# Expert results added into token rows by GpSimd's accumulating DMA, in place of stores and a gather at the end

## The chip, the cores and the metric

The kernel runs on one core of one Trainium2 chip. The metric is device time in microseconds, from the start to the end of one launch. Five engines share the work: TensorE (PE), VectorE (DVE), ScalarE (ACT), GpSimd (POOL) and SyncE (SP), which here only issues DMAs.

## The reference

One layer: 2048 tokens (16 tiles of 128) of width 512. Gated cross attention comes first, then a feed-forward part, a mixture of eight experts with widths 256 to 1024 and two experts per token:

```python
h = x @ down_w + down_b                        # 512 -> 256
probs = softmax(x @ router_w + router_b - COST_LAMBDA * cost)
topv, topi = top_k(probs, 2)
gate = softmax(topv)
for k in range(2):
    for e in range(8):                         # only the token's own expert sees h, the others see 0
        hm = h * (topi[..., k] == e)
        acc += gelu(gelu(hm) @ w1[e] + b1[e]) @ w2[e] + b2[e]
    out += acc * gate[..., k]
out += 0.1 * (gelu(gelu(h) @ shared_w1 + shared_b1) @ shared_w2 + shared_b2)
out = out @ up_w + up_b + gelu(x) @ core_w + core_b
```

What an expert gives for a zero row is a constant, so the kernel runs each expert only on its own tokens and adds the constants by a small matrix product.

## The kernel before, in words

Every product is made of three float16 matmuls (`three`, L1124: high by high, high by low, low by high), which stand for one in float32. The order of the work on each engine is written out by hand in lists (`seq`), and engines wait for each other on semaphores whose values are planned ahead (`Tally.plan`, `wait`). Each engine and each DMA queue works in order: what stands behind a waiting instruction waits too.

**Attention** fills the first 380 us and is not changed.

**Rounds** (about 380 to 511 us). Four rounds `r`, each of four tiles of tokens. A round computes h, the logits, the top two, the gates `gat` (`g1`, `g2`), the matrix of gates `Gp` (`G`, L1544), the shared expert, and `core`. ACT copies the gelu of h of each tile as a float16 row (high and low halves, 1024 bytes; `row`, L1384), and POOL scatters each tile's rows twice, once for each of a token's two experts, into the table `g_rows` in memory, sorted by expert (`sc`, L1847: two indirect DMAs per tile, eight per round). ACT copies the shared expert's result into `acc` (L1395), 16 tiles of 256 columns in SBUF. In rounds 0 and 3 two of the row buffers lie in the part of `acc` that this copy writes, so it waits until their scatters have landed. In the last round DVE works out tables of where every block lies (`ro`, `wo`, `bo`, `flag`), and SP fills the ends of the experts' regions with zeros (L1079, L1082).

**Expert stage** (511.8 to 732.7 us). 42 half blocks `j`: 256 rows of one expert by up to 512 of its hidden columns. SP loads a block transposed (`load`, L1093), up to three ahead, into four buffers `XA`. PE computes `hidden(j)` (24 matmuls of 256 columns into `EH`), ACT takes the gelu (L1431), POOL casts it to its high half (L1910), DVE subtracts to get the low half (L1745), and PE computes `output(j)` (24 matmuls of 256 columns into `Y`). PE's order is hidden(j), output(j-1), hidden(j+1), output(j), and so on. DVE's `collect` (L1833) writes y to `ysb`, with the former half block added where both belong to one block (`flag`), and SP stores it to `y_rows` (L1104). In between DVE works out `places`, the row of `y_rows` that holds each token's result (`locate`), one small operation per half block, and SP loads back eight of the sixteen tiles of the residual (`xb_rows`, L1107).

**Final stage** (from 732.7 us). In four groups `g` of four tiles: POOL gathers for every tile the two expert rows of each token from `y_rows` (L1919: 32 indirect DMAs of 128 rows in all), DVE multiplies them by the gate and adds them to `acc` (`combine`, L1774), PE transposes `acc` (L1320, 8 transposes per group), ACT and DVE split it into halves (L1441, L1757), PE multiplies by `up_w` (24 matmuls of 512 columns per group, banks of `EH`), DVE adds the residual (L1765) and SP stores the tile to `out` (L1111). The gather buffers `yg` are four; the residual's last four tiles are loaded late, into buffers that group 1 used (L1115).

Of the kernel before, what the change touches and what calls it, by code (L numbers as in the profile page):

```python
# [20 lines left out]
F32 = mybir.dt.float32  # L21
# [7 lines left out]
P = 128  # L29
# [40 lines left out]
NCONST2 = 344  # L70
# [76 lines left out]
def constants():  # L147
# [17 lines left out]
    d[:, K2_BASE:K2_BASE + E] = REGION * np.arange(E)  # L165
    packed = [e + 8 * (HALVES[e] - 1) + 16 * HBASE[e] + 256 * FIRST[e] for e in range(E)]
# [646 lines left out]
def ffn(nc, c, keep, sb, ps, sem, ends, x1s, us, bcol, b2, rw, rb, upb, coreb, const, out):  # L813
# [4 lines left out]
    gsc = nc.dram_tensor("g_rows", [DUMP + BLK, 2 * LAT], F16, kind="Internal").ap()  # L818
    ysc = nc.dram_tensor("y_rows", [NJ * BLK, LAT], F32, kind="Internal").ap()
# [20 lines left out]
    slots, places, gat = A("slots", [P, NG, 2, G4], U32), A("places", [P, NG, 2, G4], U32), A("gat", [P, NG, 2, G4])  # L840
    nf, nz, ni, nb = A("nf", [P, E]), A("nz", [P, E], I32), A("ni", [P, E], I32), A("nb", [P, E], I32)
    hc = A("hc", [P, 4, 16])
    ro, wo, bo, flag = A("ro", [P, NJ], I32), A("wo", [P, NJ], I32), A("bo", [P, NJ], I32), A("flag", [P, NJ])
    bcur = A("bcur", [P, 2, 8])
    zrow = zs[:, :].bitcast(F16)
# [7 lines left out]
    row_of = lambda r, i: rows[i] if i < 2 or r else acc[:, i - 2, :].bitcast(F16)  # L853
    sah = [b2s[:, :].bitcast(F16), A("sah1", [P, L], F16)[:, :]]
    sal = [A(f"sal{i}", [P, L], F16)[:, :] for i in range(2)]
    rows = [A(f"rows{i}", [P, 2 * LAT], F16)[:, :] for i in range(2)]
# [4 lines left out]
    rows += [acc[:, 3 * G4 + i, :].bitcast(F16) for i in range(2)]  # L861
# [8 lines left out]

    xl = [uf[:, k, :] for k in range(LB)] + [flat(v).bitcast(F32)[:, k * L:(k + 1) * L] for v in (guh, gul) for k in range(2)]
    yg = [gf_[:, 0, :], gf_[:, 1, :], flat(gh).bitcast(F32), flat(gl).bitcast(F32)]
# [19 lines left out]
    t_ys = [T(f"y_out{i}", 16) for i in range(2)]  # L892
    t_yg = [T(f"y_in{i}", 16) for i in range(4)]
    t_xl = [T(f"xb_in{i}", 16) for i in range(8)]
# [7 lines left out]
    route_c = ["e1", "g1", "g2", "G1", "G2", "G"]  # L902
    tables = ["nf", "nz", "ni", "nb", "H", "c1", "c2", "c3", "ex", "dx", "A", "M1", "r1", "M2", "r2", "pki", "D", "valid",
              "e", "h", "t", "f", "b", "sub", "ro0", "ro1", "ro2", "ro", "wo0", "wo", "bo0", "bo", "flag"]
    four = lambda name: [(name, k) for k in range(4)]

    def seq(engine, r):
# [3 lines left out]
        if r == 0:  # L911
# [3 lines left out]
                "act": [("h", 0), ("h", 1)] + four("gu") + four("guh") + [("a", 0), ("a", 1)] + four("row") + [("gt", 0), ("acc", 0), ("acc", 1)],  # L915
# [48 lines left out]
    for j in range(NJ):  # L964
        t_gt[j % 4].plan(j)
        t_ys[j % 2].plan(j)
# [984 lines left out]
```

## Time and profile before

| | us |
|---|---|
| median of 3 runs (lowest to highest) | 803.62 (802.78 to 804.75) |
| the profiled execution's own time | 796.31 |
| its span, first to last instruction | 794.5 |
| PE busy in the span | 714.3 (90%) |
| DVE, ACT, POOL busy | 539.0, 462.8, 456.9 |
| mean granted TensorE clock | 0.970 |

The profile is of one execution, and all rows quoted are from it. A row of the timeline or of the chain begins with its start in us from the span's start, and its length in us. A row of the windows has from:to and the length in us; then the busy us, with the number of instructions, of PE's matmuls, PE's weight loads, DVE, ACT and POOL; then the granted TensorE clock (1.00 is 2.4 GHz, 0.50 is 1.2 GHz), the mean busy share of the 16 DMA engines, and GB/s. A busy engine counts for the time only where the others wait for it; an idle engine costs nothing where another sets the pace.

### The profile page before, as it was taken

The numbers are of one execution on the slowest core, as the hardware profiler recorded it, in microseconds if no ns is written. First come the engines' busy times: TensorE is split into PE (matmuls) and PEld (weight loads), VectorE is DVE, ScalarE is ACT, GpSimd is POOL, SyncE is SP. The second block draws the span as 40 slices with busy tenths as digits, with TensorE's granted clock in tenths as the row PEclk, the third lists the DMA queues.
The fourth block names the chain that finished last, engine by engine and source line by source line (L and its number), as shares of the span: only waits on it lengthen the run. The fifth ranks groups of instructions, "written<-read, shape, count | busy, mean of one in ns | idle before, by whom it ended". The sixth has DMA issues, their size and how long they took to land.

```text
span 794.5 us, 20245 instructions
## 1 busy us (share of the span) xinstructions
PE 714.3 (90%) x6134; PEld 384.1 (48%) x6134; DVE 539.0 (68%) x816; ACT 462.8 (58%) x969; POOL 456.9 (58%) x526
## 2 busy tenths in 40 slices
PE   1799999999999999999889998999999999998276
PEld 0122232333333332234445455588888888887132
DVE  2989999999999999987545865634444343433374
ACT  1399999999999999987345354244433444333010
POOL 4647778888888888577877676222222222221670
PEclk9999999999999999999979989999999999999588
DMA  6635656665666565443415123635454443432355
GB/s 201 222 112 178 198 190 191 202 195 193 188 194 200 188 196 178 137 142 120 173 69 180 59 106 112 168 81 120 110 115 112 120 119 109 113 102 73 96 186 203
DMA packets 118461, 118.18 MB, mean 149 GB/s; under 512 B 58356, under 2 KB 88308, under 8 KB 118392
## 3 DMA queue, kind: packets, MB, share of 16 engines
q1 hardware_dynamic: 114744, 108.75, 44.8%
q0 software_dynamic: 3072, 8.39, 3.3%
q8 instruction: 41, 0.67, 0.3%
q14 instruction: 28, 0.23, 0.1%
q10 hardware_dynamic: 576, 0.13, 0.1%
HBM read 59.70 MB, written 46.40 MB: 134 GB/s over the span
## 4 chain that ended last, share of the span: by engine, by line
PE 66%; DVE 8%; issue 8%; POOL 7%; ACT 5%; DMA 4%; SPq 0%; ACTq 0%; DVEq 0%; POOLq 0%
PE EH L1124 22%; PE Y L1124 15%; PE pv L527 11%; PE ring L514 7%; DVE mx L648 4%; PE nat L502 4%; ACT P L588 3%; POOL gf L1919 1%; DVE statx L630 1%; PE ring L546 1%; PE Y L1228 1%; DMA gh<-y_rows,places 1%; DMA q_scratch<-qhl 1%; POOL g_rows L1847 1%; PE EH L1166 1%
## 5 line engine op out<-in xcount | busy, mean ns | idle before, releaser
L648 DVE TENSOR_REDUCE mx<-nat 128x2 f32<-128x1024 f32 x256 | 298.2, 1215 | 29.2 <-PE nat L502 27.6
L588 ACT ACTIVATE P<-ring 128x512 f32<-128x512 f32 x512 | 276.2, 606 | 17.8 <-PE ring L514 10.0
L1431 ACT ACTIVATE X<-EH,bcur 128x256 f32<-128x256 f32 x168 | 85.8, 560 | 131.6 <-PE EH L1124 131.6
L527 PE MATMUL pv<-P,VT 128*32 128x256 f32 x2048 | 157.6, 391 | 0.3
L1910 POOL CAST u<-X 128x512 f16<-128x512 f32 x84 | 51.5, 613 | 174.9 <-ACT X L1431 174.9
L514 PE MATMUL ring<-QS,KS 49*128 49x512 f16 x512 | 122.8, 391 | 14.7 <-ACT P L588 13.4
L502 PE MATMUL nat<-KS,QS 48*128 48x512 f16 x512 | 110.9, 396 | 23.6 <-DMA KS<-k_scratch 15.9
L1124 PE MATMUL EH<-XA,whi 128*128 128x256 f16 x672 | 116.9, 273 | 1.2 <-DVE XB L1675 1.0
L1124 PE MATMUL Y<-whi,u 128*128 x672 | 116.9, 273 | 0.3 <-DVE u L1745 0.3
L1745 DVE TENSOR_TENSOR u<-X,u 128x512 f16<-128x512 f32 x84 | 57.8, 688 | 69.7 <-POOL u L1910 69.7
L1124 PE MATMUL EH<-XA,wlo 128*128 128x256 f16 x336 | 91.6, 273 | 0.0
L1124 PE MATMUL Y<-wlo,u 128*128 x336 | 91.6, 273 | 0.0
L514 PEld LDWEIGHTS ring<-QS,KS 49*128 49x128 f16 x512 | 31.9, 93 | 119.0 <-ACT P L588 99.2
L527 PEld LDWEIGHTS pv<-P,VT 128*32 128x32 f32 x2048 | 43.8, 108 | 90.9 <-issue 44.5
L1833 DVE SCALAR_TENSOR_TENSOR ysb<-ysb,flag,Y 128x512 f32<-128x512 f32 x42 | 31.4, 748 | 63.6 <-PE Y L1124 63.6
L1124 PEld LDWEIGHTS EH<-XA,whi 128*128 x672 | 65.8, 98 | 9.6 <-issue 2.0
L1124 PEld LDWEIGHTS Y<-whi,u 128*128 128x128 f16 x672 | 65.8, 98 | 8.2 <-issue 0.6
L502 PEld LDWEIGHTS nat<-KS,QS 48*128 48x128 f16 x512 | 26.0, 94 | 34.6 <-issue 17.3
L1660 DVE TENSOR_TENSOR ul<-uf,uh 128x512 f16<-128x512 f32 x16 | 25.4, 1637 | 19.0 <-ACT uh L1357 19.0
L1124 PEld LDWEIGHTS Y<-wlo,u 128*128 128x128 f16 x336 | 32.9, 98 | 3.8
L1124 PEld LDWEIGHTS EH<-XA,wlo 128*128 x336 | 32.9, 98 | 3.8
L1441 ACT CAST uh<-EH 128x512 f16<-128x512 f32 x8 | 4.7, 586 | 51.1 <-PE EH L1320 51.0
(265 smaller groups left out, 1057.7 us busy)
## 6 DMA issues: line engine op xcount, KB each, us to landing
y_rows<-ysb SPq DMA_DIRECT2D x42, 256.0 KB, 2.1
XA<-in_wall SPq DMA_DIRECT2D x8, 800.0 KB, 4.7
u<-in_wall SPq DMA_DIRECT2D x8, 800.0 KB, 4.3
QS<-q_scratch SPq DMA_DIRECT2D x64, 96.0 KB, 2.3
KS<-k_scratch SPq DMA_DIRECT2D x64, 96.0 KB, 2.3
X<-in_x SPq DMA_DIRECT2D x16, 256.0 KB, 2.7
X<-in_ctx_kv SPq DMA_DIRECT2D x16, 256.0 KB, 3.7
q_scratch<-qhl SPq DMA_DIRECT2D x16, 256.0 KB, 2.1
```

Of the source, the lines that this page charges most:

```text
L502: m = pe.matmul(nat[k % 2][:, a, :], QS[i][r, g, n, q0:q0 + P], KS[i][r, g, n, :], start=True, stop=True)
L514: pe.matmul(ring[place[key] % 3][:, :], KS[i][r, g, n, lb * P:lb * P + P], QS[i][r, g, n, :], start=True, stop=True).then_inc(t_ring.sem, 1)
L527: m = pe.matmul(pv[32 * j:32 * j + 32, q], VT[i][:, lb, g, j, :], Pb[4 * (s % 2) + j][:, q], start=(lb == 0 and half == 0), stop=(lb == 3) ...
L546: m = pe.transpose(ring[place[key] % 3][:, n * P:n * P + P], ct[i][:, lb * P:lb * P + P], ident)
L588: act.activation(Pb[4 * (s % 2) + j][:, :], bank[:, :], ACT.Exp).then_inc(t_use.sem, 1)
L648: dve.tensor_reduce(mx[:, k // 8, :, k % 8], nat[k % 2][:, :, :], AX.X, ALU.max).then_inc(t_max.sem, 1)
L1124: m = pe.matmul(dst, l, r, start=first and n == 0, stop=last and n == 2, skip_group_check=skip)
L1431: m = act.activation(af[j % 2][:, tile, :], EH[j % 2][:, n, s * BLK:(s + 1) * BLK], ACT.Gelu, bias=bcur[:, j % 2, tile:tile + 1], scale=bc ...
L1660: m = dve.tensor_tensor(ul[:, i, :], uf[:, i, :], uh[:, i, :], ALU.subtract)
L1745: dve.tensor_tensor(al[j % 2][:, 2 * n:2 * n + 2, :], af[j % 2][:, 2 * n:2 * n + 2, :], ah[j % 2][:, 2 * n:2 * n + 2, :], ALU.subtract).th ...
L1833: dve.scalar_tensor_tensor(out=ysb[j % 2][:, :, :], in0=ysb[1 - j % 2][:, :, :], scalar=flag[:, j:j + 1], in1=EY[j % 2], op0=ALU.mult, op1 ...
L1910: pool.tensor_copy(ah[j % 2][:, 2 * n:2 * n + 2, :], af[j % 2][:, 2 * n:2 * n + 2, :]).then_inc(t_pool.sem, 1)
```

## The change

Rows in `g_rows` become 1088 bytes: the 1024 bytes of before, then 16 float32 numbers ("meta"): the token's gates for the eight experts in the first eight, and the token's own row number in the last. ACT copies the meta part into each row buffer (`meta`, after the four `row` copies; in round 0 also after `gt`), and the scatter waits for it. DVE writes the row numbers (`Gi`). The padding rows at the ends of the regions get gates of zero and row numbers of a dump area of 256 rows (`blank`, set in round 3).

A table `y_sums` in memory, one row of 256 float32 for each token and the dump area, is first filled with `acc` (the shared part), one store per round, the last one ahead of the first block's load in SP's queue. For each half block SP loads also the meta part of the 256 rows (64 bytes each), ACT copies the column of the block's expert to `gcur` (`gates`), DVE copies the row numbers to `to` and multiplies y by the gate (in place of adding the former half block), and POOL adds the 2 x 128 rows into `y_sums` by two indirect DMAs that accumulate. As two half blocks can hold the same token, the add of half block j begins only when that of j-1 has landed.

Gone are the stores to `y_rows`, `flag`, `places` and its 14 operations, the 32 gathers and `combine`. When the last add has landed, SP loads `y_sums` into `acc` by four plain loads of 512 KB, one per group. The transposes of group g+1 now stand ahead of the products of group g; the transposes have their own banks (`Y[0]`), the products all four banks of `EH`. All twelve tiles of the residual that need it are loaded during the expert stage.

```diff
+                m = act.copy(row_of(r, i).bitcast(F32)[:, LAT:LAT + META], Gp[:, i, 0:META])       # "meta"
 # scalar: order within a round
-                cur([("a", 0), ("a", 1)] + four("row") + [("gt", 0)] + four("guh") + [("acc", 0), ("acc", 1)])
+                cur([("a", 0), ("a", 1)] + four("row") + four("meta") + [("gt", 0)] + four("guh") + [("acc", 0), ("acc", 1)])
 # scalar: round 0
-  ... four("row") + [("gt", 0), ("acc", 0), ("acc", 1)],
+  ... four("row") + [("gt", 0)] + four("meta") + [("acc", 0), ("acc", 1)],
 # gpsimd, scatter
             if name == "sc":
+                wait(pool, t_act, r, "meta", i)
                 wait(pool, t_act, r, "row", i)
 # sync
+            def sums(r):
+                wait(sp, t_act, r, "acc", 1)
+                sp.dma_start(ysum[r * G4 * P:(r + 1) * G4 * P].rearrange("(t p) c -> p t c", p=P),
+                             acc[:, G4 * r:G4 * r + G4, :]).then_inc(t_as.sem, 16)
...
-                sp.dma_start_transpose(gT[j % 4], gsc[bass.ds(at, BLK), :]).then_inc(t_gt[j % 4].sem, 16)
+                sp.dma_start_transpose(gT[j % 4], gsc[bass.ds(at, BLK), 0:LAT].bitcast(F16)).then_inc(t_gt[j % 4].sem, 16)
+                if j >= 4:
+                    sp.wait_ge(t_gc.sem, t_gc.at[j - 4,])
+                    sp.wait_ge(t_to.sem, t_to.at[j - 4,])
+                sp.dma_start(meta[j % 4][:, :, :], blocks(gsc[bass.ds(at, BLK), LAT:LAT + META])).then_inc(t_mt[j % 4].sem, 16)
...
-                wait(sp, t_dve, "E", j, "y")
-                sp.dma_start(blocks(ysc[j * BLK:(j + 1) * BLK, :]), ysb[j % 2][:, :, :]).then_inc(t_ys[j % 2].sem, 16)
...
+            for i in range(2):
+                sp.wait_ge(t_ad[i].sem, t_ad[i].value)
+            for g in range(NG):
+                r = C_GROUPS[g][0] // G4
+                sp.dma_start(acc[:, G4 * r:G4 * r + G4, :],
+                             ysum[r * G4 * P:(r + 1) * G4 * P].rearrange("(t p) c -> p t c", p=P)).then_inc(t_al[g].sem, 16)
 # scalar, after the second gelu of each half block
+        def gates(j):
+            v = act.value_load(eo[0:1, j:j + 1], min_val=0, max_val=E - 1)
+            wait(act, t_mt[j % 4], j)
+            if j >= 4:
+                wait(act, t_dve, "E", j - 4, "y")
+            act.copy(gcur[:, j % 4, :].unsqueeze(2), meta[j % 4][:, :, bass.ds(v, 1)]).then_inc(t_gc.sem, 1)
 # vector
         def collect(j):
+            wait(dve, t_mt[j % 4], j)
+            if j >= 2:
+                wait(dve, t_ad[j % 2], j - 2)
+            dve.tensor_copy(to[:, j % 2, :], meta[j % 4][:, :, META - 1]).then_inc(t_to.sem, 1)
             wait(dve, t_pe, "E", j, "y")
-            if j >= 2:
-                wait(dve, t_ys[j % 2], j - 2)
-            if j >= 1:
-                wait(dve, t_dve, "E", j - 1, "y")
-            dve.scalar_tensor_tensor(out=ysb[j % 2][:, :, :], in0=ysb[1 - j % 2][:, :, :], scalar=flag[:, j:j + 1],
-                                     in1=EY[j % 2], op0=ALU.mult, op1=ALU.add).then_inc(t_dve.sem, 1)
+            dve.wait_ge(t_gc.sem, t_gc.at[j,])
+            dve.tensor_tensor(ysb[j % 2][:, :, :], EY[j % 2], gcur[:, j % 4, :].unsqueeze(2).broadcast_to([P, 2, LAT]),
+                              ALU.mult).then_inc(t_dve.sem, 1)
 # gpsimd
+            def add(j):
+                wait(pool, t_dve, "E", j, "y")
+                pool.wait_ge(t_to.sem, t_to.at[j,])
+                if j >= 1:
+                    wait(pool, t_ad[(j - 1) % 2], j - 1)
+                else:
+                    pool.wait_ge(t_as.sem, t_as.value)
+                    pool.wait_ge(t_dz.sem, 16)
+                for a in range(2):
+                    pool.indirect_dma_start(out=ysum[:, :], out_offset=bass.IndirectOffsetOnAxis(ap=to[:, j % 2, a:a + 1], axis=0),
+                                            in_=ysb[j % 2][:, a, :], in_offset=None, compute_op=ALU.add).then_inc(t_ad[j % 2].sem, 16)
             for j in range(NJ):
...
                     pool.tensor_copy(ah[j % 2][:, 2 * n:2 * n + 2, :], af[j % 2][:, 2 * n:2 * n + 2, :]).then_inc(t_pool.sem, 1)
+                if j >= 1:
+                    add(j - 1)
+            add(NJ - 1)
```

## Rows read from the trace of the kernel before

**Rows 1.** Windows: the expert stage, the gap before the final products, the rest.

```profile
511.80:732.65 220.85, 220.32 (x2015) 197.01 (x2016) 87.88 (x140) 89.31 (x209) 51.52 (x84) 1.00 0.43 107
732.65:749.39 16.74, 0.27 (x3) 0.00 (x0) 4.63 (x9) 0.00 (x0) 9.70 (x11) 0.62 0.29 86
749.39:794.50 45.11, 33.20 (x128) 15.34 (x128) 27.16 (x48) 4.69 (x8) 21.01 (x22) 0.80 0.55 183
```

**Rows 2.** The chain that ended last, one period of the expert stage.

```profile
619.77 2.62 PE EH L1124 x24
622.39 2.62 PE Y L1124 x24
```

**Rows 3.** The same chain in the final stage.

```profile
736.64 1.00 POOL gf L1919
...
784.10 7.17 PE EH L1124 x24
791.29 0.75 DVE uf L1765
```

**Rows 4.** Line L1919, the gathers: from issue to landing.

```profile
DMA to landing us min/median/max: 2.7/2.8/4.6
```

**Rows 5.** Line L1847, the scatters: ns of one (min/median/max), first and last start.

```profile
L1847 POOL DMA_INDIRECT g_rows<-rows,slots x16: 956/964/1431, 391.4 to 496.4; - x16
...
DMA to landing us min/median/max: 2.4/3.1/6.4
```

**Rows 6.** Timeline, VectorE and GpSimd in one period of the expert stage.

```profile
625.05 0.75 DVE L1833 SCALAR_TENSOR_TENSOR ysb<-ysb,flag,Y 128x512 f32<-128x512 f32 x1 [1.51 <-PE Y L1124]
625.71 0.68 DVE L1745 TENSOR_TENSOR u<-X,u 128x512 f16<-128x512 f32 x1
...
627.44 0.61 POOL L1910 CAST u<-X 128x512 f16<-128x512 f32 x1 [3.31 <-ACT X L1431]
```

**Rows 7.** Timeline, round 1: a scatter's issue beside a VectorE operation.

```profile
425.88 1.43 POOL L1847 DMA_INDIRECT g_rows<-rows,slots  x1 [0.28 <-issue]
...
425.63 0.69 DVE L1670 SCALAR_TENSOR_TENSOR sal<-ysb,sah 128x512 f16<-128x512 f32 x1 [0.51 <-POOL sah L1839]
```

**Rows 8.** Timeline, round 0: two of ACT's copies.

```profile
392.66 0.58 ACT L1387 COPY GT<-EH 32x512 f32<-32x512 f32 x1 [2.75 <-PE EH L1212]
403.07 1.07 ACT L1395 COPY acc<-Y 128x512 f32<-128x512 f32 x2 [9.83 <-DMA g_rows<-acc,slots]
```

**Rows 9.** Timeline, round 3 up to the expert stage.

```profile
492.42 1.10 POOL L1847 DMA_INDIRECT g_rows<-rows,slots  x1 [0.28 <-ACT rows L1384]
...
492.40 1.07 ACT L1384 COPY acc<-Y 128x512 f16<-128x512 f16 x2
504.99 1.07 ACT L1395 COPY acc<-Y 128x512 f32<-128x512 f32 x2 [6.94 <-DMA g_rows<-acc,slots]
...
505.83 5.24 SPq L1093 DMA_TRANSPOSE XA<-g_rows  x3
...
511.81 0.28 PE L1124 MATMUL EH<-XA,whi 128*128 128x256 f16 x1 [1.03 <-DVE XB L1675]
```

**Rows 10.** DMA issues: what, count, KB each, median us to landing.

```profile
XA<-in_wall SPq DMA_DIRECT2D x8, 800.0 KB, 4.7
...
X<-in_x SPq DMA_DIRECT2D x16, 256.0 KB, 2.7
...
XA<-g_rows SPq DMA_TRANSPOSE x42, 3.2
```

**Rows 11.** Timeline, PE in the final stage, first at half clock, then at full.

```profile
749.42 1.94 PE L1320 MATMUL EH<-cst,acc 128*128 128x128 f32 x8 [16.50 <-DVE acc L1774]
...
753.66 0.39 PE L1124 MATMUL EH<-wlo,uh 128*128 128x512 f16 x1
...
760.14 1.77 PE L1320 MATMUL EH<-cst,acc 128*128 128x128 f32 x8 [1.99 <-DVE XB L1765]
...
767.39 0.38 PE L1124 MATMUL EH<-whi,ul 128*128 128x512 f16 x1
```

More of the change, by code:

```diff
@@ L852, in ffn @@
     sah_of = lambda r, i: sah[i] if i or r else lp[:, :].bitcast(F16)[:, 0:L]
-    row_of = lambda r, i: rows[i] if i < 2 or r else acc[:, i - 2, :].bitcast(F16)
+    row_of = lambda r, i: rows[i] if i < 2 or r else firsts[i - 2]
     sah = [b2s[:, :].bitcast(F16), A("sah1", [P, L], F16)[:, :]]
     sal = [A(f"sal{i}", [P, L], F16)[:, :] for i in range(2)]
-    rows = [A(f"rows{i}", [P, 2 * LAT], F16)[:, :] for i in range(2)]
+    rows = [A(f"rows{i}", [P, ROW // 2])[:, :].bitcast(F16) for i in range(2)]
     guh, gul = A("guh", [P, LB, L], F16), A("gul", [P, LB, L], F16)
@@ L860, in ffn @@
     acc = A("acc", [P, B, LAT])
-    rows += [acc[:, 3 * G4 + i, :].bitcast(F16) for i in range(2)]
+    quarter = lambda r: acc[:, G4 * r:G4 * r + G4, :].rearrange("p t c -> p (t c)").bitcast(F16)
+    rows += [quarter(3)[:, i * ROW:(i + 1) * ROW] for i in range(2)]
+    firsts = [quarter(0)[:, i * ROW:(i + 1) * ROW] for i in range(2)]
     sa = [y[:, :, :].rearrange("p a c -> p (a c)") for y in ysb]
@@ L1435, in rest @@
                         columns(j + 1)
-            for g in range(NG):
-                for n in range(2):
+                    elif n == 1:
+                        gates(j)
+            for kind, g in C_STEPS:
+                for n in range(2 if kind == "ot" else 0):
                     wait(act, t_pe, "C", g, "ot", n)
@@ L1540, in route @@
                 return dve.tensor_tensor((Ga, Gb)[n][:, :, :], (m1, m2)[n][:, :, :], wide(gat[:, r, n, :]), ALU.mult)
+            if what == "Gi":
+                wait(dve, t_pe, r - 1, "gt", 0)
+                wait(dve, t_act, r - 1, "meta", G4 - 1)
+                return dve.tensor_copy(Gp[:, :, META - 1], cs2[:, K2_ID + G4 * r:K2_ID + G4 * r + G4])
             if what == "G":
@@ L1543, in route @@
                 wait(dve, t_pe, r - 1, "gt", 0)
+                wait(dve, t_act, r - 1, "meta", G4 - 1)
                 return dve.tensor_tensor(Gp[:, :, 0:E], Ga[:, :, :], Gb[:, :, :], ALU.add)
@@ L1764, in rest @@
                         wait(dve, t_xl[where[t][1]], t)
-                    dve.scalar_tensor_tensor(out=dst, in0=cbank(g, "fin", i), scalar=gate[:, 4:5], in1=dst,
+                    dve.scalar_tensor_tensor(out=dst, in0=H[i], scalar=gate[:, 4:5], in1=dst,
                                              op0=ALU.mult, op1=ALU.add).then_inc(t_dve.sem, 1)
-        def combine(g):
-            for i, t in enumerate(C_GROUPS[g]):
-                wait(dve, t_yg[i], "C", g)
-                for k in range(2):
-                    if k == 1:
-                        wait(dve, t_dve, "C", g, "y1", i)
-                    dve.scalar_tensor_tensor(out=acc[:, t, :], in0=yg[i][:, k * LAT:(k + 1) * LAT],
-                                             scalar=gat[:, t // G4, k, t % G4:t % G4 + 1], in1=acc[:, t, :],
-                                             op0=ALU.mult, op1=ALU.add).then_inc(t_dve.sem, 1)
```

256 lines of the change are left out of this document (98 added, 158 removed).

## The prediction, made before the result was known

> **What bounds the kernel now.** I read the windows first, cut where the chain of waits changes its character. In the expert stage PE is busy for 220.3 of 220.85 us at full clock [rows 1]; the chain there is nothing but 24 matmuls of hidden and 24 of output in turn, 2.62 us each, a period of 5.24 us for each of 42 half blocks [rows 2]. Nothing else limits this stage, so a new operation on another engine is free as long as it fits into 5.24 us. From 732.65 on it is another kernel: 16.7 us with PE idle, then 45.1 us in which PE is busy for 33.2 at a mean clock of 0.80 [rows 1]. The chain there enters POOL's 32 gathers at 736.64 [rows 3], each of which keeps POOL for about 1.0 us and 0.3 until the next, as a scatter does [rows 3, 5, 7], some 40 us in all, and PE works in bursts between them. That tail, 61.85 us to the span's end, is what the change can shorten. The gathers and combine go with it.
>
> **The change part by part.**
>
> *The tail.* Call T the end of the last output (732.65). The product by the gate costs DVE as much as the operation that it replaces, 0.75 us [rows 6], done at T+1.05. The add of half block 40 can begin at about T-2.0, for output 41 follows output 40 directly, 2.62 us long [rows 2], with a short stall; its second DMA is issued 1.26 us later (0.96 and 0.30 [rows 5, 7]) and lands L after that, where L is an accumulating DMA's time from issue to landing. The trace has none. Nearest are the scatter of the same 128 rows of 1 KB, 2.4 to 6.4 us, median 3.1 [rows 5], and the gather, 2.7 to 2.8 mostly, 4.6 at most [rows 4]. An accumulate must read the row in memory and write it. I take 3.1 and 0.4 (the gather's median less the quickest scatter, for the read), L = 3.5, with 2.4 and 6.4 as ends. Add 40 has landed at T+2.8, add 41 begins at 2.9, issues its second half at 4.15 and has landed at T+7.65. SP then issues four loads of 512 KB. Between 2.7 us for 256 KB and 4.7 for 800 KB [rows 10] 512 KB takes 3.6, and each further one 1.9 more. Group 0 is there at T+11.4, group 1 at 13.3. Their transposes at half clock take 1.94 us each [rows 11], so the first product starts at T+15.4. Four groups of 24 matmuls of 512 columns at twice 2.62/24 = 0.218 us [rows 2] are 21.0, two more sets of transposes at full clock 1.0 each (half of 1.94). DVE needs 4 x 0.75 and two splits of 0.68 per group [rows 6], 4.4 us, less than PE's 6.2, so PE sets the pace.
>
> Clock: before, the first burst became fast 4.2 us after its start (749.42 to 753.66), the second 7.2 after (760.14 to 767.39), and the last 24 matmuls again took 7.17 where 5.24 is the full clock's [rows 3, 11]. The new tail is one unbroken burst, so only its start is slow: 0 to 1.6 us, I take 0.8. From PE's end to the span's end it is 3.2 us as before (791.3 to 794.5) [rows 3]. Sum: 15.4 + 21.0 + 2.0 + 0.8 + 3.2 = 42.4 against 61.85, a gain of 19.4, give or take 2.5 for landings beside the stores. It moves with L by 2 us for each us.
>
> *Round 0.* The scatters wait for meta, which in this round stands behind the copy of GT, 392.66 + 0.58 [rows 8], instead of starting at 391.4 [rows 5]. With a meta copy of 0.2 (much smaller than GT's 0.58; my estimate) the first starts at about 393.5, 2.1 later. ACT's copy of acc waits for the landing of the last one (9.83 us of idle time end there [rows 8]), and the chain goes on through it: +2.1. In rounds 1 and 2 the four small copies fit into ACT's wait for the transposed gates, and nobody waits for the scatters: 0 (at most 0.8 each).
>
> *Start of the expert stage.* In round 3 the scatters start behind the row copies (492.40 + 1.07) and one meta copy, 1.2 after 492.42. The acc copy moves from 504.99 to 506.2, ends at 507.3, and SP's store of it, 512 KB, now stands ahead of the first transposing load, which goes from 505.83 to 507.9. It lands 3.2 later [rows 9, 10], or about 2 more behind the store's bytes: 511.1 to 513. PE is ready at 511.8 by its core products [rows 9]. So 0 to 1.3; I take 0.5.
>
> *Work in the expert stage.* ACT is busy for 89.3 of 220.9 us [rows 1], 2.1 in a period, and gets one copy of 2 numbers per partition; DVE keeps its load; SP loses a store and gets the small load of meta. Its transposing loads now wait, behind the meta load, for DVE's `to`; that delays them by under 2 us, and they run three half blocks (15.7 us) ahead of a need of 3.2: 0. POOL gets 2 issues. They begin when y is written, 625.05 + 0.75, and end 2.2 us later, at 628.0; the cast that stood at 627.44 [rows 6] moves by 0.9. Its result is due at the output that starts at 632.87 (622.39 and two periods [rows 2]), four microseconds after: covered. Uncovered, it would cost 0.9 in each period, 38 us.
>
> *The chain of adds.* What is new is that add j waits for the landing of add j-1. Its own period is 0.96 + 0.30 (first issue) + L + 0.1 (my allowance for the semaphore) = L + 1.36, and if that is over 5.24 it sets the pace of POOL, then of the casts and of PE: the limit is L = 3.88. With L = 3.5 it is 4.86, hidden. Behind a waiting add on POOL stand both casts of the next half block, so there is no way round it. One effect eats the slack: an issue that began at 425.88, during a DVE operation with two inputs in SBUF, took 1.43 us instead of 0.96 [rows 7], and the new first issue falls on just such an operation (625.71) [rows 6]. Then the chain is 0.47 longer, 5.33, and costs 41 x 0.09 = 3.7. I take 2, between 0 and 3.7.
> The Trainium skill states this as a rule (SBUF — State Buffer, Who interferes with whom): a VectorE instruction with two SBUF inputs contends with a GpSimd instruction that reads SBUF. By that rule the longer chain holds in all periods, and the sum gains 2 us less than with the middle; without it, 2 us more.
>
> Sum: -19.4 + 2.1 + 0.5 + 2 = -14.8. The profiled execution's 796.3 would become 781.5; its own time is 7.3 below the median of the runs, and I take the difference over: 803.6 - 14.8 = 789.
>
> **The rivals.**
>
> *B, the chain of adds becomes the bound, slower than before.* For it: L's spread of 2.4 to 6.4 [rows 5], an accumulate does more than a scatter, and the DMA engines are 43% busy in this stage [rows 1], with the transposing load just ahead of the add. Against: the quiet scatters landed in 2.4. Price: 41 x (L - 3.88) and 2 x (L - 3.5) in the tail; it decides from L = 4.25, where it has eaten the 16.8. At L = 4.8 it is 37.7 + 2.6 against 16.8: 827. At 6.4: 103 and more, near 896.
>
> *C, the tail stays bound by transfers.* 2 MB of loads and 4 MB of stores must pass; the stores come every 1.3 us with 256 KB. If the loads land one behind the other as late as 4.7 each, group 3 comes at T+27, still before its turn, but the first two cost 4 more, and stores that queue another 3 at the end: 796. Against it: the windows show a DMA share of only 0.55 in the tail of before.
>
> *D, the transposing loads become slow.* Source rows lie 1088 bytes apart instead of 1024. No row shows such a pitch. They have 15.7 us for 3.2, so it needs a factor of four to reach PE; then it is 5 to 10 us, about 797.
> The Trainium skill says that a descriptor that does not start on a 256-byte boundary is cut into one more access (DMA: Bandwidth & Descriptors, How a descriptor splits into AXI transactions); three of four rows would do so here. No run here shows it yet.
>
> *E, it does less than it says*: L near 2.4 makes all hidden and the tail 2.2 better; 785. It belongs to the forecast.
>
> **How the numbers follow.** Forecast with E 0.52; B 0.36 (0.32 of it slower than before, 0.02 within, 0.02 faster); C 0.08 and D 0.04 (together 0.08 faster, 0.02 and 0.02). The likeliest one's own range is 783 to 797. The range: below, 803.6 - 19.4 - 2.2 + 2.6 is 784.6, less 1.5 for quicker loads, 783. Above, it takes in B up to L = 5.0, which is 835, and leaves out about one in ten there. 0.3% (2.4 us) is what a measurement can tell from no change. Faster by more: 0.52 + 0.02 + 0.08 = 0.62. Within: 0.02 + 0.02 = 0.04. Slower: 0.32 + 0.02 = 0.34.
>
> **What would show it.** Right: 24 matmuls in 2.62 us throughout the expert stage; POOL's add waits for DVE's y, not for a DMA; landing of adds 3 to 3.8 us; about 42 us from PE's last output to the end; the first scatter of round 0 two microseconds later. Wrong: PE idle in each period, with casts late and POOL's idle time ended by the DMA of the adds; the period then reads L + 1.36 or L + 1.8. C shows as PE waiting for acc's loads, D as hidden(j) waiting for the XA loads.

## The result: 4.6% slower, where 1.8% faster was forecast

| | before | after |
|---|---|---|
| median, 4 runs each on one chip (lowest to highest) | 803.42 (802.78 to 804.75) | 840.55 (837.75 to 842.70) |
| ratio, 95% interval | | 1.0458 (1.0422 to 1.0493) |
| the profiled execution's own time | 796.31 | 842.70 |
| its span | 794.5 | 840.6 |

The windows of the changed kernel, cut at PE's first hidden matmul and the end of its last output, answer to [rows 1] (columns as there):

```profile
516.50:796.20 279.70, 233.41 (x2016) 195.59 (x2016) 97.31 (x167) 92.85 (x251) 177.54 (x166) 0.98 0.61 92
796.20:840.60 44.40, 28.11 (x129) 14.72 (x128) 17.86 (x25) 4.49 (x8) 3.08 (x2) 0.80 0.48 151
```

The same 2016 matmuls now take 279.70 us instead of 220.85, and PE is idle for 46.3 of them; POOL's busy time in the stage has grown from 51.5 to 177.5. The granted clock is 0.98 instead of 1.00 now that PE pauses. The two cuts give the whole balance of the spans: the stage starts 4.7 us later, is 58.85 longer, and the tail behind it falls from 61.85 to 44.4, a gain of 17.45. 4.7 + 58.85 - 17.45 = 46.1 = 840.6 - 794.5. The medians differ by 37.1 only: before's profiled execution was 7.1 us quicker than the median of its four runs and is none of them, after's was 2.2 slower than its median. So some 9 us of the balance lie between executions and not in the change; the traces locate 1.5 of them. Of the 4.7, 1.5 is no effect of the change: ACT's copy of GT in round 0 starts at 394.16 instead of 392.66 [rows 8], ahead of anything new.

Where PE's idle time comes from, in the view of waits over the stage (engine, what it waited for: us in total, times, longest):

```profile
PE Y L1141 <- DVE u L1772: 46.1, 36, 3.6
```

DVE's low half is late in 36 of 42 half blocks (the other 13 us of the stage's growth are PE's own busy time, which is up from 220.3 to 233.4). That low half waits in its turn for POOL (page of the changed kernel, costliest groups; the last item is the idle time and who ended it):

```profile
L1884 POOL DMA_INDIRECT y_sums<-ysb,to x84 | 130.9, 1559 | 99.0 <-DVE u L1772 45.5
L1772 DVE TENSOR_TENSOR u<-X,u 128x512 f16<-128x512 f32 x84 | 72.7, 866 | 180.7 <-POOL u L1892 180.7
```

So by these views POOL waits for DVE, and DVE for POOL: a loop. And each accumulating DMA keeps POOL for 1.56 us, where the scatter takes 0.96 [rows 5]. One period in the timeline of the two engines:

```profile
639.92 1.56 POOL L1884 DMA_INDIRECT y_sums<-ysb,to  x1 [1.86 <-DVE u L1772]
641.79 1.54 POOL L1884 DMA_INDIRECT y_sums<-ysb,to  x1 [0.30 <-PE Y L1141]
642.77 1.74 POOL L1892 CAST u<-X 128x512 f16<-128x512 f32 x2
646.26 1.56 POOL L1884 DMA_INDIRECT y_sums<-ysb,to  x1 [1.75 <-DVE ysb L1802]
...
643.99 1.07 DVE L1772 TENSOR_TENSOR u<-X,u 128x512 f16<-128x512 f32 x1 [4.10 <-POOL u L1892]
644.99 0.16 DVE L1799 CAST to<-meta 128x2 uint32<-128x2 f32 x1
645.06 0.68 DVE L1802 TENSOR_TENSOR ysb<-Y,gcur 128x512 f32<-128x512 f32 x1
```

Read it as a ring. The first add issue (1.56), 0.30, the second (1.54) and the first cast (0.64) fill POOL from 639.92 to 643.97. Only then can DVE take the low half of the next half block (1.07), which stands ahead of `collect` in DVE's order. `collect` makes ysb (done at 645.74), and 0.52 later POOL starts the next add. 1.56 + 0.30 + 1.54 + 0.64 + 0.02 + 1.07 + 0.68 + 0.52 = 6.33, and the adds stand 6.34 apart. PE needs 5.24. (POOL's own view puts the wait for the second issue down to PE; it is the 0.30 between two issues, as everywhere.)

The last term is not the ring's. Beside it lies a second limit, the chain of landings: the add of half block j waits until the second DMA of j-1 has landed. The trace keeps the time of each landing, and with it the two candidates can be told apart (us from the span's start; the last row is e3 below, where no add waits for the one just before it):

| half block | ysb done | second DMA of the one before landed | first DMA starts | after ysb | after the landing |
|---|---|---|---|---|---|
| 17 | 639.29 | 639.16 | 639.92 | 0.63 | 0.76 |
| 18 | 645.74 | 645.50 | 646.26 | 0.52 | 0.76 |
| 21 | 665.13 | 666.54 | 667.30 | 2.17 | 0.76 |
| 38 | 779.51 | 779.14 | 779.90 | 0.39 | 0.76 |
| e3, 18 | 641.92 | - | 642.20 | 0.28 | - |

In 39 of the 41 periods the add starts 0.76 or 0.77 us after the landing (0.84 and 1.49 in the other two), while the distance from ysb goes from 0.36 to 2.17. Where DVE is the last that POOL waits for, in e3, that distance is 0.28 in 39 of 41. So the landing sets every period of the changed kernel, 1.56 + 0.30 + landing + 0.76, and the ring by itself is 6.33 - 0.52 + 0.28 = 6.09, just hidden behind it. The second DMA lands 3.50 to 5.36 us after its start, 3.83 in the median, 4.0 on average; the median period is 6.47, the mean 6.63, the shortest 6.12. 41 x (6.63 - 5.24) = 57 us is the loss of the stage (279.7 us against 222.5 in e1).

The views name DVE all the same, because they go by the event that came last, and ysb or the second low half often ends between the landing and POOL's start. The first fence is the landing of the adds, first and second DMAs together (view of line L1884), the second POOL's waits in the stage, which name a landing only five times:

```profile
DMA to landing us min/median/max: 3.5/3.9/5.6
```

```profile
POOL y_sums L1884 <- DVE u L1772: 45.5, 23, 2.5
POOL y_sums L1884 <- DVE ysb L1802: 22.3, 13, 1.9
...
POOL y_sums L1884 <- DMA y_sums<-ysb,to: 15.6, 5, 3.4
```

The start of the stage, SP's queue (answers to the third group of [rows 9]), and a piece of the chain:

```profile
494.96 12.84 SPq L1091 DMA_DIRECT2D g_rows<-u  x8
507.84 0.47 SPq L1092 DMA_DIRECT2D y_sums<-u  x1
508.64 1.71 SPq L1073 DMA_DIRECT2D y_sums<-acc  x1
513.19 1.37 SPq L1105 DMA_TRANSPOSE XA<-g_rows  x1
...
516.58 0.39 PE L1141 MATMUL EH<-XA,whi 128*128 128x256 f16 x1 [3.89 <-DMA XA<-g_rows]
```

```profile
507.84 4.51 DMA y_sums<-u
```

SP waits for the landing of the dump store (507.84, 4.51 long in the chain) before the first load, at 513.19; PE then waits 3.89 us for it. Before, the first load went at 505.83 and PE was held by its own work.

The tail, from the chain that ended last (start, length, what), answers to [rows 3]:

```profile
792.76 1.56 POOL y_sums L1884
...
794.62 3.50 DMA y_sums<-ysb,to
...
798.88 1.54 POOL y_sums L1884
800.42 0.30 POOLq L201
800.72 3.83 DMA y_sums<-ysb,to
...
804.62 4.04 DMA acc<-y_sums
808.66 0.04 issue
808.71 1.13 PE Y L1336 x4
...
813.26 6.82 PE EH L1141 x24
```

### The profile page after: what moved, and what is told of

It reads as the page before. It is cut to its first block, busy times and chain, and to the rows that moved or that the text cites. A ratio compares the mean times of both kernels' runs of the same rounds, so it can differ in the third digit from the quotient of the medians.

```text
span 840.6 us, 20788 instructions
## 1 busy us (share of the span) xinstructions
PE 720.8 (86%) x6134; PEld 380.1 (45%) x6134; DVE 535.0 (64%) x815; ACT 467.8 (56%) x1027; POOL 557.1 (66%) x578
## 4 chain that ended last, share of the span: by engine, by line
PE 49%; issue 13%; DVE 13%; POOL 12%; DMA 5%; ACT 5%; SPq 2%; ACTq 0%; DVEq 0%; POOLq 0%
PE EH L1141 11%; PE pv L532 11%; PE Y L1141 9%; POOL y_sums L1884 7%; PE ring L519 7%; PE nat L507 4%; DVE mx L653 4%; DVE u L1772 4%; ACT P L593 3%; POOL u L1892 3%; DMA y_sums<-ysb,to 1%; DVE statx L635 1%; PE ring L551 1%; DMA rbb<-in_rb 1%; DVE ysb L1802 1%
## 5 line engine op out<-in xcount | busy, mean ns | idle before, releaser
L1884 POOL DMA_INDIRECT y_sums<-ysb,to x84 | 130.9, 1559 | 99.0 <-DVE u L1772 45.5
L1772 DVE TENSOR_TENSOR u<-X,u 128x512 f16<-128x512 f32 x84 | 72.7, 866 | 180.7 <-POOL u L1892 180.7
L1141 PE MATMUL Y<-whi,u 128*128 x672 | 122.5, 280 | 46.2 <-DVE u L1772 46.1
L1141 PE MATMUL Y<-wlo,u 128*128 x336 | 93.9, 280 | 0.0
L532 PEld LDWEIGHTS pv<-P,VT 128*32 128x32 f32 x2048 | 43.9, 108 | 90.8 <-issue 44.6
L1892 POOL CAST u<-X 128x512 f16<-128x512 f32 x84 | 72.0, 1157 | 16.9 <-ACT X L1454 16.9
L1141 PEld LDWEIGHTS EH<-XA,whi 128*128 x672 | 66.2, 98 | 13.7 <-issue 4.4
L1836 POOL TENSOR_TENSOR pexp<-cst,lg 128x16 f32<-128x16 f32 x8 | 25.0, 3120 | 11.3 <-DVE lg L1499 11.2
```

The costliest lines, as they stand in the source:

```text
L532: m = pe.matmul(pv[32 * j:32 * j + 32, q], VT[i][:, lb, g, j, :], Pb[4 * (s % 2) + j][:, q], start=(lb == 0 and half == 0), stop=(lb == 3) ...
L1141: m = pe.matmul(dst, l, r, start=first and n == 0, stop=last and n == 2, skip_group_check=skip)
L1772: dve.tensor_tensor(al[j % 2][:, 2 * n:2 * n + 2, :], af[j % 2][:, 2 * n:2 * n + 2, :], ah[j % 2][:, 2 * n:2 * n + 2, :], ALU.subtract).th ...
L1836: m = pool.tensor_tensor(pe_[:, two, :], base[:, 0:2 * E].rearrange("p (t e) -> p t e", t=2), lg[:, two, :], ALU.pow)
L1884: pool.indirect_dma_start(out=ysum[:, :], out_offset=bass.IndirectOffsetOnAxis(ap=to[:, j % 2, a:a + 1], axis=0), in_=ysb[j % 2][:, a, :], ...
L1892: pool.tensor_copy(ah[j % 2][:, 2 * n:2 * n + 2, :], af[j % 2][:, 2 * n:2 * n + 2, :]).then_inc(t_pool.sem, 1)
```

## The experiments

"After" is the changed kernel. Each ratio is to the kernel before, run on the same chip (its medians were 794.3 to 802.3 on the chips used). Spans and periods are from the profiled execution. Theory P: the ring of POOL and DVE. Theory W: the chain of landings.

**e1: only the last two adds.** The adds of half blocks 0 to 39 are left out; everything else of the change stays.

```diff
             def add(j):
+                if j < NJ - 2:
+                    return
```

> Leaves out the adds of half blocks 0 to 39 (no DMA issued for them, no wait on them); the last two stay. All theories: the expert stage is again PE's, 42 x 5.24 = 220 us instead of 280, so about 842 - 59 = 783 us. It shows what the start of the stage and the tail are worth by themselves. If the period stays above 5.3 us, neither the issues nor the landings are the cause.

Measured: 786.27 us, ratio 0.9788 (0.9764 to 0.9811), span 784.4, period 5.24. Windows from 530 to 735:

```profile
530.00:735.00 205.00, 205.00 (x1880) 183.75 (x1878) 80.33 (x156) 86.06 (x233) 48.21 (x79) 1.00 0.34 66
```

PE is busy for all of the 205 us. The whole loss is in the adds. The transposing loads from rows 1088 bytes apart, the loads of meta, ACT's and DVE's new copies cost PE nothing, and rival D is out: a transposing load lands after 3.3 us in the median here, 3.2 before.

**e2: the same issues without accumulating** (the sums are left out of the result).

```diff
-  in_=ysb[j % 2][:, a, :], in_offset=None, compute_op=ALU.add).then_inc(...)
+  in_=ysb[j % 2][:, a, :], in_offset=None).then_inc(...)
```

> The adds become plain scatters of the same rows (a later half block overwrites, sums are left out of the result); waits, order and count as in the changed kernel. If accumulating is the cause of both limits, an issue takes 0.96 instead of 1.56 us and lands after 3.1 instead of 3.9: loop over DVE 0.96 x 2 + 0.3 + 0.66 + 1.07 + 0.6 + 0.35 = 4.9 us, landing chain 0.96 + 0.3 + 3.1 + 0.5 = 4.9 us, both under PE's 5.24, total 784 to 790 us. Rival: the landings are late because of the other transfers in this stage, not because they accumulate; then the period is 5.6 to 6.2 and the total 800 to 825 us.

Measured: 797.63 us, ratio 0.9938 (0.9911 to 0.9964), span 795.4. POOL's timeline:

```profile
642.68 0.98 POOL L1884 DMA_INDIRECT y_sums<-ysb,to  x1 [4.08 <-DMA y_sums<-ysb,to]
...
647.61 1.18 POOL L1884 DMA_INDIRECT y_sums<-ysb,to  x1 [1.50 <-DVE ysb L1802]
649.10 0.96 POOL L1884 DMA_INDIRECT y_sums<-ysb,to  x1 [0.30 <-issue]
...
653.97 0.98 POOL L1884 DMA_INDIRECT y_sums<-ysb,to  x1 [2.74 <-DMA y_sums<-ysb,to]
```

An issue takes 0.96 again, and where DVE is the releaser the period is 4.93: the ring with short issues fits into 5.24. So the length of the issue decides about P. But longer periods, mostly 6.0 to 7.7, alternate with it, where a plain scatter landed late (POOL's waits in the window from 530 to 735 name a landing 11 times, 35.7 us). The time lies between the two expectations. Of the 56.2 us of span that e1 wins back from after, this wins 45.2.

**e3: two tables.** Odd half blocks add into a second table (left out of the result), so that an add waits for the one before last.

```diff
-                if j >= 1:
-                    wait(pool, t_ad[(j - 1) % 2], j - 1)
-                else:
+                if j >= 2:
+                    wait(pool, t_ad[j % 2], j - 2)
+                elif j == 0:
...
-                    pool.indirect_dma_start(out=ysum[:, :], ...
+                    pool.indirect_dma_start(out=(ysum, ysum2)[j % 2][:, :], ...
```

> Adds of odd half blocks go to a second table (whose sums are left out of the result), so an add waits for the landing of the add two half blocks back. Theory W (the wait for the landing sets the period): the period of 6.6 us falls to about 5.4, total 790 to 795 us. Theory P (a loop of two issues of 1.56 us, cast, split, collect and back to the next add, 3.4 + 0.64 + 1.07 + 0.75 + 0.6 = 6.46 us): no change, 836 to 842 us.

Measured: 826.90 us, ratio 1.029 (1.0265 to 1.0315), span 826.6. Neither expectation was met: P had forecast no change, W 790 to 795. What is left is P alone:

```profile
641.24 0.68 DVE L1803 TENSOR_TENSOR ysb<-Y,gcur 128x512 f32<-128x512 f32 x1
...
642.20 1.75 POOL L1885 DMA_INDIRECT y_sums<-ysb,to  x1 [1.50 <-DVE ysb L1803]
...
648.48 1.75 POOL L1885 DMA_INDIRECT y_sums<-ysb,to  x1 [1.51 <-DVE ysb L1803]
...
654.77 1.75 POOL L1885 DMA_INDIRECT y_sums<-ysb,to  x1 [1.51 <-DVE ysb L1803]
```

No landing is waited for in the stage, the period is 6.28 or 6.29 in all but a few, and POOL starts 0.28 after ysb. With the landings out of the way the ring stands next, only 0.35 us shorter than after's mean period of 6.63: that is why removing the limit that set the pace gives 14 us and no more (41 x 0.35). The stage is still 43.9 us longer than in e1 (266.4 against 222.5).

**e4: collect first.** One table; DVE makes ysb of j-1 before the low halves of j.

```diff
                 if j < NJ:
+                    if j >= 1:
+                        collect(j - 1)
                     for n in range(2):
                         wait(dve, t_pool, "E", j, n)
...
-                        if n == 0 and j >= 1:
-                            collect(j - 1)
```

> DVE's order changed only: the gated product of y(j-1) stands ahead of the split al(j,0), so that it no longer waits for POOL's cast. Theory P: the loop is cut and the next limit shows, 1.56 + 0.3 + 3.9 + 0.1 to 0.6 = 5.9 to 6.4 us per half block, total 805 to 830 us. Theory W: no change, 836 to 842 us.

Measured: 848.92 us, ratio 1.0583 (1.054 to 1.0625), span 847.1. Both expectations missed: P had forecast a gain (805 to 830), W no change (836 to 842), and it came out 1.2% slower than after. The ring is open, and the chain of landings alone sets the period, 6.52 here, 6.63 in the median, 6.83 on average; landing of all adds 3.6/4.3/6.3 us (min/median/max):

```profile
643.33 1.56 POOL L1884 DMA_INDIRECT y_sums<-ysb,to  x1 [2.21 <-DVE to L1799]
645.20 1.54 POOL L1884 DMA_INDIRECT y_sums<-ysb,to  x1 [0.30 <-issue]
...
649.85 1.56 POOL L1884 DMA_INDIRECT y_sums<-ysb,to  x1 [1.93 <-DVE to L1799]
```

From 645.20 to 649.85 it is 4.65: a landing of 3.89 and again 0.76, as in 39 of its 41 periods. A kernel that gains nothing when its ring is opened was not held by the ring. That it even loses 8 us lies in the landings: the second DMAs land 0.2 us later on average than in after (4.18 against 3.97), times 41; why they do, no run shows. (The releaser named, `to`, is that of the next half block, which waits for the same landing in DVE's `collect`.)

**e5: both**, the edits of e3 and e4 together (again without the second table in the result).

> Both edits (two tables, of which the second is left out of the result, and DVE's order). Theory P: with both limits gone POOL's own work is left, 3.4 + 0.6 + 1.3 = 5.3 us per half block, total 784 to 792 us, well below either edit alone. Theory W: the same as with two tables alone.

Measured: 783.38 us, ratio 0.9769 (0.9735 to 0.9802), span 779.3; timeline, and windows from 530 to 735:

```profile
645.08 1.75 POOL L1885 DMA_INDIRECT y_sums<-ysb,to  x1 [0.45 <-DVE ysb L1803]
...
650.32 1.75 POOL L1885 DMA_INDIRECT y_sums<-ysb,to  x1 [0.46 <-DVE ysb L1803]
```

```profile
530.00:735.00 205.00, 203.43 (x1864) 182.11 (x1863) 86.42 (x158) 86.09 (x233) 174.74 (x157) 1.00 0.84 116
```

That is P's forecast, less 0.6 us, and not W's. Period 5.24, PE busy for 203.4 of 205, although POOL has the same work per half block as in after. In medians, one edit alone gave -13.7, the other alone +8.4, both together -57.2. Both limits are shown: landings, mean period 6.63, which set the pace, and the ring, 6.1 to 6.3, close behind. The second hid what the removal of the first was worth.

**e6: the start.** The dump store goes into round 1, and the last store of the sums behind the first three loads.

```diff
-            sp.dma_start(blocks(ysum[ROWS:ROWS + BLK, :]), blank[:, :, 0:LAT]).then_inc(t_dz.sem, 16)
-            sums(NG - 1)
...
             for j in range(3):
                 load(j)
+            sums(NG - 1)
```

> The changed kernel with two stores taken from the way of the first block's load: the dump area of y_sums is filled in round 1, and round 3's store of acc stands behind the first three loads. Theory S (SP's wait for the dump store's landing, 4.5 us, delays the stage): the first matmul of the stage moves from 516.5 to about 513.5, total 3 us less than the changed kernel, 837 us. Rival: the scatters' landing or PE's core products hold it; then under 1 us less.

Measured: 838.37 us, ratio 1.0484 (1.0436 to 1.0532), span 836.0.

```profile
507.75 1.46 SPq L1107 DMA_TRANSPOSE XA<-g_rows  x1
...
513.11 0.28 PE L1144 MATMUL EH<-XA,whi 128*128 128x256 f16 x1 [1.03 <-DVE XB L1705]
```

The first hidden matmul starts 3.5 us earlier than in after and is released by DVE's product, as before the change. 1.4 of that is not the edit's: ACT's copy of GT in round 0 starts at 392.72 instead of 394.16. And in the seven other runs with after's opening (e1 to e5, e9, e10) PE waits 1.6 to 4.0 us for this load, where it waits 1.03 for DVE here. The trace confirms the place of this loss; its size is 0.6 to 3 us. The edit moves two stores at once and doesn't say what each is worth. The ratios of e6 and after overlap, so in the time it is not shown: 3 us is inside what they can tell.

**e9 and e10: no transposing loads beside the adds.** e4 and e2, without the transposing loads of half blocks 4 and later (old data are used, so the sums are others). They ran on a chip where the kernel before took 794.7 us, not 802, so the expected times fit less well than ratios, periods and landings.

```diff
-        t_gt[j % 4].plan(j)
+        if j < 4:
+            t_gt[j % 4].plan(j)
...
+                if j < 4:
                     sp.dma_start_transpose(...)
```

> The one-table kernel with the collecting products ahead of the gating of the next half block (848.9 us), without the transposing loads of half blocks 4 and later: the first tiles' data are used again, so the output is not the reference's. In it the period is issue to issue of one chain: 0.30 + 1.54 us, the landing of the second add, and about 0.5 us to start again. Theory: the landings are long (4.3 us median) because these loads share the DMA engines; without them they land in about 3.5 us, the period is 1.86 + 3.5 + 0.5 = 5.9 us instead of 6.8, 809 us (800 to 820). Rival: an accumulating add takes 4 us or more by itself, with or without other transfers: 840 to 850 us, landing median 4.1 to 4.4.

Measured: 833.75 us, ratio 1.0478 (1.0446 to 1.0511), span 832.6, landing 3.6/3.8/5.2.

```profile
636.69 1.56 POOL L1887 DMA_INDIRECT y_sums<-ysb,to  x1 [1.85 <-DVE to L1802]
...
643.00 1.56 POOL L1887 DMA_INDIRECT y_sums<-ysb,to  x1 [1.73 <-DVE to L1802]
```

Between the two expectations: the period is 6.31 here, 6.42 in the median and 6.47 on average (6.83 in e4), and the median landing half a microsecond shorter than in e4, which is the part that the loads have in it. By ratio it is 1% faster than e4. 3.8 us is what an accumulating add takes even then, with the DMA engines' share down from 0.59 to 0.44.

> The kernel whose scatters store without accumulating (797.6 us; the sums are left out of the result), without the transposing loads of half blocks 4 and later too. Theory: the long ones of its alternating periods (6.4 us beside 4.9) are landings that stand behind a transposing load; without these loads every period is TensorE's 5.24 us, 780 us (777 to 785). Rival: the long periods come from the loop between GpSimd and VectorE, not from the loads: 795 to 800 us.

Measured: 781.34 us, ratio 0.9818 (0.9784 to 0.9853), landing 2.4/2.6/3.8, PE busy for 204.8 of 205 us, and a median period of 5.24 (two of 41 are 5.9 and 6.1):

```profile
636.17 1.17 POOL L1887 DMA_INDIRECT y_sums<-ysb,to  x1 [1.63 <-DVE ysb L1805]
...
641.41 1.17 POOL L1887 DMA_INDIRECT y_sums<-ysb,to  x1 [1.64 <-DVE ysb L1805]
```

The theory held: e2's long periods were landings behind these loads. Without them a plain scatter lands in 2.6, and an add in 3.8, both from the start of the issue: about 1.2 us is the accumulating itself, half of it the issue that is 0.6 longer.

**e7, e8, e11, e12: a version that beats both.** Two tables, both initialised, collect first, the start of e6; SP loads both tables back and DVE adds them:

```diff
+                sp.dma_start(dst, (ysum, ysum2)[i][r * G4 * P:(r + 1) * G4 * P]...).then_inc((t_al, t_bl)[i][g].sem, 16)
...
+            def merge(g):
...
+                dve.tensor_tensor(part, part, other[g], ALU.add).then_inc(t_dve.sem, 1)
```

e7 loads the whole even table while the last odd add is under way.

> A complete version: two tables, the second filled with zeros in round 1, DVE's product ahead of the split, the start as in e6_start, and at the end the even table loaded while the last odd add is under way and the two added on DVE. From the 783 of both edits: 4 less at the start, 1 less because the last add does not wait for the one before, 2 more for the first merge (1.2 us) and the loads: about 780 us (776 to 784). Rival: POOL, busy for 5.2 of 5.24 us in each period, tips over, or DVE's merges stall PE in the final stage: 787 to 797 us.

Measured: 787.21 us, ratio 0.9817 (0.979 to 0.9845), span 787.3. That is the rival's range. POOL did not tip over (every period but a few is 5.24); the excess is in the tail, 48.5 us from the last output's end against 41.8 in e5.

```profile
741.61 1.54 POOL L1910 DMA_INDIRECT y_sums<-ysb,to  x1 [0.30 <-issue]
...
741.19 2.27 SPq L1139 DMA_DIRECT2D acc<-y_sums  x4
749.74 0.91 SPq L1139 DMA_DIRECT2D X<-y_sums  x2
```

The add issued at 741.61 had landed only at 749.7, 8.1 us later, beside four loads of 512 KB. e8 puts two of the four behind it:

```diff
-            for i in range(2):
-                sp.wait_ge(t_ad[i].sem, t_ad[i].value)
-                for g in range(NG):
+            for i, g in [(0, 0), (0, 1), (1, 0), (1, 1), (0, 2), (1, 2), (0, 3), (1, 3)]:
+                if g == 0:
+                    sp.wait_ge(t_ad[i].sem, t_ad[i].value)
```

> The merged version (two tables, collect first, zero stores late, even table read back and added by VectorE), with only the order of SP's last loads changed: tiles 0 and 1 of the even table before the last odd add has landed, then tiles 0 and 1 of the odd table, then tiles 2 and 3 of both. If the last odd add landed 8.1 us after its issue because four loads of 512 KB stood in front of it, two loads ahead of it cost it less: landing in 4 to 5 us, the tail some 3 to 5 us shorter, 783 us (781 to 785). If the transfer as a whole bounds the tail (2 MB more to read at the end), the order changes nothing: 786 to 788 us, with the last merge at the same distance from the last ysb product.

Measured: 783.94 us, ratio 0.9856 (0.983 to 0.9883), span 785.4. The time is in the first range, the landing is not (4 to 5): it took 6.2 us (742.58 to 748.83) and the end came 45.6 us behind the last ysb product instead of 48.5: 2.9 us of tail in the trace, of which a repeat of the same kernel (e12) shows 1.9. Its ratio, on another chip, is no better than e7's, so the times don't show a gain. e11 holds all eight loads until the landing:

```diff
+            for i in range(2):
+                sp.wait_ge(t_ad[i].sem, t_ad[i].value)
-            for i, g in [(0, 0), (0, 1), (1, 0), (1, 1), (0, 2), (1, 2), (0, 3), (1, 3)]:
-                if g == 0:
-                    sp.wait_ge(t_ad[i].sem, t_ad[i].value)
+            for i, g in [(0, 0), (1, 0), (0, 1), (1, 1), (0, 2), (1, 2), (0, 3), (1, 3)]:
```

> The merged version again, with none of SP's last eight loads issued before the last odd add has landed, and then tile by tile from both tables. The last odd add (1.54 us of issue, then its rows) landed 8.1 us after the start of its issue behind four loads of 512 KB, and 6.2 us behind two. With none ahead it should land in 3.6 to 4.3 us, the first merge on VectorE should come some 2 us earlier than with two loads ahead (13.1 us from the last ysb product to the first merge there), and the tail shrink by 0 to 2 us: 782 to 784 us beside 784 us for the version with two ahead. Rival: the eight loads (4 MB) bound the tail by their volume, so that two of them moved behind the landing cost as much as the landing gains: no change, or 1 to 2 us more.

> The version with two loads ahead of the last landing once more, on the chip of the one with none ahead, for a direct comparison of their tails: last add landed 6.2 us after its issue, first merge 13.1 us behind the last ysb product, span end 45.6 us behind it; 784 us within the 1 % by which chips differ.

Measured, both on one chip: e11 785.99 us, ratio 0.9896 (0.9872 to 0.9921); e12 784.40, ratio 0.987 (0.9851 to 0.9889). e11's add landed in 3.8 (739.19 to 742.99) and the first merge came 12.5 us behind the last ysb product instead of 13.0 (748.89 behind 736.38; 749.89 behind 736.92), but the second merge had to wait again and the end came no earlier (47.0 and 46.6 us behind it). No gain, as the rival had it: it fits that the volume of the loads sets this tail, not the last landing. (All these landings are taken up to SP's next load, which waits for them.) The merged versions are 1.0 to 1.8% faster than the kernel before.

## Why the prediction was wrong, step by step

*The step that failed: "0.96 + 0.30 (first issue) + L + 0.1 (my allowance for the semaphore) = L + 1.36 ... With L = 3.5 it is 4.86, hidden."* The chain of adds was not hidden, it set every period of the stage: 1.56 + 0.30 + 4.0 + 0.76 = 6.6 us on average against PE's 5.24. Three of its four terms were too small: the first issue by 0.60 (it was sized by the scatter, 0.96; an accumulating one took 1.54 to 1.56 where no such DVE operation ran beside it, and 0.96 without the accumulating, e2), the landing by 0.5, the start behind the landing by 0.66. Only the landing had been given a range. L = 3.5 itself was the minimum. The allowance of 0.4 for the read was the small term: e10 against e9 says 1.2, the longer issue included.

The mechanism had been named, as rival B with 0.36, and it is what happened (e4, e5). But its limit of L = 3.88 was too kind: by these terms it is 5.24 - 1.86 - 0.76 = 2.6, under the quickest add seen (3.5), so one table can't reach PE's pace here at all. The case written down for B was one of long landings, from L = 4.25. The time, 840.55, lies above the range (835), which priced only L.

*A second step failed behind it: "POOL gets 2 issues. They ... end 2.2 us later ... the cast ... moves by 0.9 ... covered."* The issue was too short here too. (By its own numbers, 628.0 less 627.44, the cast moves by 0.6; 0.9 holds only with a pause of 0.3 behind the issues.) And the step ended at the output that needs the cast, without asking who else is behind it. DVE's low half of the next half block waits for that cast, `collect` stands behind the low half on DVE, and the next add waits for `collect`. That closes a ring whose length is POOL's and DVE's work in series, not each one's load against 5.24: 6.09 us with issues of 1.56, 6.28 in e3 with 1.75. With issues of 0.96 it would be 6.09 - 0.60 - 0.58 = 4.91, and e2's short periods are 4.93. Had the chain of landings been as short as forecast, this ring alone would have cost 42 x 1.04 = 43.7 us, e3's period against PE's. "Uncovered, it would cost ... 38 us" was the right order of size, written beside the wrong verdict.

*The issue beside DVE.* "The new first issue falls on just such an operation", 0.47 more: where it does, in e3 and e5 (on DVE's second low half, which follows the product), it takes 1.75 instead of 1.54, 0.21 more; in after the landing holds it until that operation is nearly over, and it takes 1.56. The same goes on between cast and low half: DVE's low half takes 1.07 beside POOL's second cast and 0.68 alone, and that stands in the ring.
The Trainium skill (SBUF — State Buffer, Who interferes with whom) names such a pair, a VectorE instruction with two SBUF inputs and a GpSimd one that reads SBUF. For the low half beside the cast the trace agrees, with 0.39 us. For the issue of a DMA the trace shows 0.21, though the same section takes such an issue to be untouched by a `tensor_tensor`, as something inferred; here the measurement decides.

*The tail was right.* 44.4 us against 42.4, a gain of 17.45 against 19.4. The add of half block 40 landed at T+1.9 (2.8 forecast), 41 at T+8.35 (7.65), the transposes started at T+12.5 (11.4), the first product at T+17.1 (15.4), and from there to the last product's end 24.1 (23.8). The excess of 2.0 builds up as 0.7 to the last landing (0.6 for the longer first issue, 0.33 for the landing, less the earlier start of the add), 0.4 for the first load (4.04 instead of 3.6), 0.6 for the first two sets of transposes and 0.3 in the products. The clock's term was 1.6, the upper end, and not 0.8: the first 24 matmuls took 6.82 where 5.24 is the full clock's. Rival C did not come: the four loads landed at T+12.5, 13.9, 15.4 and 16.9, the last three each before its turn. The term that failed in the stage, the restart of 0.76, stands here too, behind the landing of add 40.

*Round 0 was right:* the first scatter of after starts at 395.15, 3.75 behind [rows 5], less 1.5 of drift 2.25 (2.1 forecast); the copy of acc 406.84 instead of 403.07 [rows 8], less the drift 2.27 (2.1). Little of it is left in round 3: ACT's copy of acc's row buffers starts at 494.31 instead of 492.40 [rows 9], 0.4 beyond the drift.

*Start of the stage was too small:* +0.5 (0 to 1.3) against 4.7 less 1.5, some 3, of which 0.4 came along from round 0. That is one run: PE's wait for this load varies from 1.6 to 4.0 us over the runs with the same opening. I counted the store of acc ahead of the first load and not the store of the dump rows, whose landing SP waits for; e6 takes that wait away.

*The transposing loads (rival D) and "0" for meta's loads and the small copies:* right for PE (e1, 205.00 of 205.00). The transposing loads are not free for the adds: they lengthen landings by half a microsecond (e9).
The Trainium skill's rule that a descriptor off a 256-byte boundary is cut into one more access (DMA: Bandwidth & Descriptors, How a descriptor splits into AXI transactions) is not tested apart by any run here; with the pitch of 1088 bytes the transposing loads land after 3.3 us in e1, 3.2 before, and PE's time is the same.

*What stays open:* what in the accumulating DMA makes POOL's issue 0.6 us longer. Why five of after's landings take 4.6 to 5.4 us (e9, without the transposing loads, has one above 4.5), and why e4's are longer than after's. And what the 0.76 from a landing to POOL's next issue consists of, against 0.28 behind a DVE product.

## What to carry to other kernels

When an order between DMAs is added, the chain of issue, landing and restart is a limit of its own: price each term, with a range for each. When work is added to an engine, don't compare its load with the period either; follow what each added instruction releases until you are back at it, and add up the ring with the order in which each engine issues. When two limits lie near each other, undo both together before you judge either: here one edit alone gave 14 us, the other alone cost 8, the pair gave 57. And don't take the releaser that a view names for the limit when two events lie within a microsecond of each other: look over many periods for the distance that stays the same. Here it was 0.76 behind the landing, while the view named DVE.

## What the runs showed that I had not expected

- An indirect DMA that accumulates keeps GpSimd for 1.54 to 1.56 us per 128 rows of 1 KB; the same without accumulating 0.96. Landing (median, from the start of the issue) 3.8 against 2.6 without the transposing loads, 3.9 to 4.3 with them.
- A small indirect DMA lands late beside large loads: 3.8 us after the start of its issue with none, 6.2 with two of 512 KB, 8.1 with four.
- From a landing to the next issue on POOL it took 0.76 us, in 39 of 41 periods of after, e4, e6 and e9 alike; from the end of DVE's product 0.28.
- With the DMA engines' share at 0.84 in e5, twice that of before (0.43), PE was idle for only 1.6 us in 205, in a single wait for DVE.
